# A transformer stack in one kernel: the top-1 expert stages send finished groups home by scatter, with parts of 3 and 5 batches

## The chip, the cores and the metric

The kernel runs on one core of a Trainium2 chip. The metric is the device time of one execution in microseconds (us). TensorE is PE, VectorE DVE, ScalarE ACT, GpSimd POOL and SyncE SP, as in the profile.

## The reference

The input x is 8 batches of 512 tokens of 128 numbers. Eight layers follow each other, each added to x: RWKV mixing, top-1 experts, attention with 16 heads, top-1 experts, attention with a Laplacian function, top-2 experts, Mamba, top-2 experts. The change touches the two top-1 expert layers, which use the same weights:

```python
x = x + _L0_ffn_ref(_layernorm(x, axis=-1), W1, b1, W2, b2, Wr, br)
...
logits = x @ Wr + br                     # 8 experts
idx = jnp.argmax(logits, axis=-1)
probs = jax.nn.softmax(logits, axis=-1)
gates = jnp.take_along_axis(probs, idx[..., None], axis=-1)[..., 0]
for ei in range(e):
    h = jax.nn.gelu(xf @ W1[ei] + b1[ei], approximate=False)
    y = h @ W2[ei] + b2[ei]
    mask = (idxf == ei).astype(xf.dtype)
    out = out + y * (gf * mask)[:, None]
```

W1 is 128 by 512 for each expert and W2 is 512 by 128, all in fp32. Each token uses one expert, chosen by the data.

## The kernel before

x lies in SBUF for the whole program. The stages run one after the other, `STAGES = [RWKV, TOP1, HEADS, TOP1, LAPLACE, TOP2, MAMBA, TOP2]`. At the end of each stage every engine but SP drains and adds to one semaphore, and all wait for the sum of the four (`between`, L1898 to L1901). The order within a stage is written out by hand, engine by engine; semaphores join the engines.

An expert stage (`sorted_tensor`, `sorted_scalar`, `sorted_vector`, `sorted_pool`, `sorted_sync`, L244 to L564) sorts tokens by expert so that each group of 128 rows has one expert. The 8 batches are cut into parts (`PARTS`, L212; for top 1 two parts of 4 batches, 16 tiles of 128 tokens each). For each part:

- DVE takes the statistics (`statistics`), POOL the inverse deviations (L516), DVE normalises into `xn` (L375). PE turns the tiles (L252) and computes the logits (L267), DVE chooses the expert (`route`) and computes each token's place in the sorted order (`places`), with which the index tile is done (L446). A part with n tiles has n + 7 groups, since every expert's rows are rounded up to whole groups; the surplus rows are padding.
- POOL scatters the normalised tiles to the sorted tensor in DRAM by one indirect DMA each (`scatter`, L522).
- SP loads the sorted rows in chunks of up to four groups into a ring of three (`load`, L552). PE turns them; for each group DVE copies the expert's weights (128x1156) into one of five slots (`fill_slot`, L459), PE computes the first layer (L285), ACT the GELU (L329), PE the second layer (L293), and DVE adds b2 into `ys` (`keep`, L466). Part 0 has 23 groups and part 1 too, 46 in all in 12 chunks; they run through in one loop.
- SP stores each finished chunk in sorted order (`store`, L557). When all chunks of a part have landed, POOL gathers each tile of tokens by an indirect DMA (`gather`, L533), and DVE adds it, times its gate, to x (`add`, L474). After batch 0 DVE takes the next stage's first statistics (`take_statistics`). All adds stand behind the whole loop of groups in DVE's order.

When HEADS comes next, ACT ends its part by filling two buffers of that stage with constants (`heads_fill`, L753 and L754), once the last group's second layer is done. POOL ends a stage with the normalisation of the next stage's batch 0 (L172 to L180), unless that is an expert stage.

At the start of the program SP issues the first loads, waits for POOL's `s.filled`, and then issues the loads that later stages need. ACT, also behind `s.filled`, takes one exponential (`decay_scalar`, L1613), on which DVE waits before it mixes RWKV's weights (L1617 to L1624), which PE awaits.

## Time and profile before

| | |
|---|---|
| Median of 3 runs | 2268.59 us (2267.01 to 2269.56) |
| The profiled execution's own time | 2265.75 us |
| Its span | 2264.0 us, mean granted clock 0.828 |
| Busy: PE, DVE, ACT, POOL | 1647.6 (73%), 1665.7 (74%), 1054.8 (47%), 1049.0 us (46%) |
| POOL, indirect scatters `sorted_x<-xn,index` (L522) | 192, busy 195.1 us |
| POOL, indirect gathers `yg<-sorted_y,index` (L533) | 192, busy 194.6 us, idle before them 171.3 us |

A busy time is the sum over instructions. The two indirect lines cover both top-1 stages (32 of each per stage) and both top-2 stages (64 per stage). In a timeline row stand the start, the duration (of the whole run of equal instructions where xN is over 1), the engine and the line; in brackets the idle time before and what ended it.

### The profile page before, as it was taken

To read this page: it belongs to the slowest core of one execution; us is meant where nothing else is said; L and a number is where in the kernel's file an instruction comes from. 1 tells how busy PE (TensorE), PEld (TensorE's weight loads), DVE (VectorE), ACT (ScalarE), POOL (GpSimd) and SP (SyncE) were. 2 spreads that over 40 slices of the span, in tenths; PEclk is the share of its full clock that TensorE was granted. 3 is DMA by queue.
4 is the path that set the end of the run, shared out by engine and by line. 5 is a ranking of instruction groups with operands and counts; after the bars stand their busy time and mean duration, and the time that the engine had idled before them with its cause. 6 is when DMAs were issued, how large, how long until landed. Compare 5 with 4: busy or idle time off the path is not lost. (4 is left out here: it accounts for less than half of the span.)

```text
span 2264.0 us, 28290 instructions
## 1 busy us (share of the span) xinstructions
PE 1647.6 (73%) x8402; PEld 974.4 (43%) x8402; DVE 1665.7 (74%) x3318; ACT 1054.8 (47%) x2009; POOL 1049.0 (46%) x845
## 2 busy tenths in 40 slices
PE   5636935899999985945635943887988888885692
PEld 2326931233333325943435941443443443343692
DVE  7985546888888825546766662899999999997664
ACT  3433640566666771626832632534434444431361
POOL 5636331222222005352207771567666666574776
PEclk8656966999999995977765976988987997896696
DMA  8012315333333201212002530000000000000363
GB/s 248 1 6 69 86 35 63 40 43 45 44 41 44 32 2 46 83 55 61 0 1 76 163 104 33 0 1 1 1 1 0 0 1 0 0 0 12 101 167 107
DMA packets 141594, 102.53 MB, mean 45 GB/s; under 512 B 16360, under 2 KB 133360, under 8 KB 141328
## 3 DMA queue, kind: packets, MB, share of 16 engines
q1 hardware_dynamic: 129168, 75.72, 15.9%
q0 software_dynamic: 12288, 25.19, 3.8%
q8 instruction: 60, 0.98, 0.2%
q14 instruction: 78, 0.64, 0.1%
HBM read 42.92 MB, written 38.27 MB: 36 GB/s over the span
## 5 line engine op out<-in xcount | busy, mean ns | idle before, releaser
L1520 POOL TENSOR_TENSOR m_hc<-m_state,bc 128x512 f32<-128x512 f32 x256 | 378.2, 1477 | 216.9 <-DVE m_state L1463 216.9
L931 DVE TENSOR_REDUCE maxima<-banks 128x1 f32<-128x512 f32 x512 | 320.2, 681 | 46.9 <-PE banks L781 45.8
L1390 ACT ACTIVATE banks<-banks,rates 128x512 f32<-128x512 f32 x256 | 168.8, 661 | 342.7 <-PE banks L1236 342.2
L889 ACT ACTIVATE h_p<-banks 128x512 f32<-128x512 f32 x512 | 274.0, 597 | 113.6 <-PE banks L789 112.5
L1463 DVE TENSOR_TENSOR_SCAN m_state<-banks,m_drive 128x512 f32<-128x512 f32 x256 | 310.1, 1212 | 22.9 <-ACT banks L1390 20.4
L533 POOL DMA_INDIRECT yg<-sorted_y,index x192 | 194.6, 1014 | 171.3 <-DMA sorted_y<-ys 105.3
L329 ACT ACTIVATE hid<-banks,slot 128x128 f32<-128x128 f32 x708 | 211.4, 367 | 110.1 <-PE banks L285 109.8
L522 POOL DMA_INDIRECT sorted_x<-xn,index x192 | 195.1, 1016 | 90.0 <-issue 57.1
L781 PE MATMUL banks<-ks,qs 128*128 128x512 bf16 x512 | 204.8, 402 | 40.8 <-DMA qs<-nothing 22.5
L285 PE MATMUL banks<-xt,slot 128*128 128x128 f32 x1416 | 212.4, 286 | 11.7 <-DVE slot L459 9.8
L293 PE MATMUL banks<-slot,hid 128*128 128x128 f32 x1416 | 201.1, 276 | 0.0
L466 DVE TENSOR_TENSOR ys<-banks,slot 128x128 f32<-128x128 f32 x262 | 76.4, 292 | 162.3 <-PE banks L293 160.3
L789 PE MATMUL banks<-qs,ks 128*128 128x512 bf16 x512 | 191.1, 382 | 4.2 <-ACT h_p L889 2.3
L285 PEld LDWEIGHTS banks<-xt,slot 128*128 128x128 f32 x1416 | 184.6, 198 | 20.7 <-issue 15.9
L1227 PE MATMUL banks<-high,choose 128*128 128x512 f32 x256 | 147.9, 578 | 59.0 <-DVE m_drive L1457 42.0
L293 PEld LDWEIGHTS banks<-slot,hid 128*128 128x128 f32 x1416 | 180.0, 193 | 0.0
L1457 DVE TENSOR_TENSOR m_drive<-banks,bc 128x512 f32<-128x512 f32 x256 | 171.6, 670 | 11.2 <-PE banks L1228 11.1
L984 POOL TENSOR_TENSOR h_less<-less_rest,zero 8x512 bf16<-8x512 f32 x16 | 16.5, 1028 | 327.1 <-DVE less_rest L938 327.1
L321 ACT ACTIVATE xt<-banks 128x512 f32<-128x512 f32 x100 | 58.7, 587 | 216.3 <-PE banks L252 214.7
L1235 PE MATMUL banks<-high,choose 128*128 128x512 f32 x256 | 126.1, 493 | 44.9 <-DVE m_state L1463 44.2
L781 PEld LDWEIGHTS banks<-ks,qs 128*128 128x128 bf16 x512 | 50.0, 98 | 222.2 <-DVE maxima L931 160.6
L798 PE MATMUL banks<-h_p,h_v 128*32 128x512 f32 x1024 | 136.4, 605 | 5.8 <-ACT h_p L889 5.5
(253 smaller groups left out, 3030.6 us busy)
## 6 DMA issues: line engine op xcount, KB each, us to landing
xg<-sorted_x SPq DMA_DIRECT2D x58, 256.0 KB
sorted_y<-ys SPq DMA_DIRECT2D x58, 256.0 KB
qs<-part SPq DMA_DIRECT2D x144, 64.0 KB
ks<-part SPq DMA_DIRECT2D x144, 64.0 KB
sorted_x<-zeros SPq DMA_DIRECT2D x3, 1984.0 KB, 15.6
t1w<-in_t1w SPq DMA_DIRECT2D x16, 256.0 KB, 5.9
sorted_x<-xn,index POOLq DMA_INDIRECT x192, 2.2
yg<-sorted_y,index POOLq DMA_INDIRECT x192
```

Source lines behind the costliest of these rows:

```text
L285: last = pe.matmul(m.bank[2 + g % 3][:, n * P:(n + 1) * P], f.slot[:, g % SLOT_RING, n * P:(n + 1) * P], x, start=True, stop=True)
L293: last = pe.matmul(m.bank[5 + g % 3][:, 0:P], f.hid[:, g % 3, n, :], f.slot[:, g % SLOT_RING, (NB + n) * P:(NB + n + 1) * P], start=n == 0 ...
L329: act.activation(f.hid[:, g % 3, n, :], m.bank[2 + g % 3][:, n * P:(n + 1) * P], f.func, bias=bias).then_inc(f.hidden, 1)
L522: pool.indirect_dma_start(f.xs[p][0:part.groups * P, :], bass.IndirectOffsetOnAxis(ap=f.index[:, v:v + 1], axis=0), f.xn[:, part.tile + n ...
L533: pool.indirect_dma_start(f.yg[:, v, :], None, f.yd[p][0:part.groups * P, :], bass.IndirectOffsetOnAxis(ap=f.index[:, v:v + 1], axis=0)).t ...
L781: pe.matmul(m.bank[bank][:, :], f.qs[:, h, head, tile * P:(tile + 1) * P], f.ks[:, h, head, :], start=True, stop=True).then_inc(f.ring_mad ...
L789: pe.matmul(m.bank[5 + item % SHIFTED_BANKS][:, :], f.ks[:, h, head, tile * P:(tile + 1) * P], f.qs[:, h, head, :], start=True, stop=True) ...
L889: act.activation(f.p[:, slot % 2, j, :], m.bank[5 + item % SHIFTED_BANKS][:, :], ACT.Exp, scale=1.0 / math.sqrt(HD)).then_inc(f.exps, 1)
L931: dve.reduce_max(f.maxima[:, tile, head:head + 1], m.bank[bank][:, :], AX_X).then_inc(f.ring_read, 1)
L1457: dve.tensor_tensor(f.drive[:, n % 4, :], m.bank[4 + n % 2][:, :], f.bc[:, b[1] % 2, 0, :], ALU.mult).then_inc(f.driven, 1)
L1463: dve.tensor_tensor_scan(f.state[:, n % 4, :], m.bank[2 + n % 2][:, :], f.drive[:, n % 4, :], 0.0, ALU.mult, ALU.add).then_inc(f.states, 1)
L1520: pool.tensor_tensor(f.hc[:, n % 8, :], f.state[:, n % 4, :], f.bc[:, now[1] % 2, 1, :], ALU.mult).then_inc(f.weighed, 1)
```

## The change

The top-1 stages (`f.back` = 1) work as follows; the top-2 stages keep their way.

- A row of the sorted tensor has 129 numbers: the 129th is the token's number as an integer. POOL makes the numbers once (`m.ids`); at the stage's head DVE copies them behind the rows of `xn`. The scatter carries them along. Each use has row tensors of its own in DRAM, filled at the start with padding rows: ACT writes a zero block `m.pads`, POOL numbers it from 4096 on, and SP stores it four times, behind `s.filled` 2.
- When a chunk is there, DVE copies its numbers into `f.home`, 128x4 (`noted`). A later load into the same place of the ring waits for that too.
- `ys` has room for all 46 groups. As soon as a group is kept, POOL scatters it to `m.home`, in the tokens' order (`send_back`). When all groups of a part are sent, SP loads its batches plainly (`fetch`), up to three at a time.
- Parts have 3 and 5 batches (19 and 27 groups). DVE adds part 0's batches after group 40 of 46 (`EARLY_ADDS` = 6), with the next stage's first statistics, and part 1's after the loop.
- The masks for `places` now exist for four sizes instead of two. In the head stage one semaphore takes the place of another.

```diff
 EXPERTS = 8
-PARTS = {1: (4, 4), 2: (2, 3, 3)}
+PARTS = {1: (3, 5), 2: (2, 3, 3)}
+ROW = P + 1
+EARLY_ADDS = 6
 STEPS = {(1, 2): 42, (2, 3): 107}
-CONSTANTS = 5
-HEADS_GAP = 3392
+CONSTANTS = 7
+HEADS_GAP = 3096
 SLOT_RING = 5
...
         activate(g)
     if f.fill:
         act.wait_ge(f.second, f.base.second + len(f.groups))
+        act.wait_ge(f.noted, f.base.noted + len(f.chunks) * f.back)
         for p, part in enumerate(f.parts):
             act.wait_ge(f.scattered[p], f.base.scattered[p] + 16 * part.lanes)
         heads_fill(act, m, f.fill)
...
     def keep(g):
         c, t = f.groups[g]
-        if t == 0 and c >= 3:
+        if f.back and t == 0:
+            chunk = f.chunks[c]
+            dve.wait_ge(f.loaded[c % 3], f.base.loaded[c % 3] + 16 * (c // 3 + 1))
+            dve.tensor_copy(f.home[:, g:g + chunk.size], f.xg[:, c % 3, 0:chunk.size, P].bitcast(U32)).then_inc(f.noted, 1)
+        if not f.back and t == 0 and c >= 3:
             dve.wait_ge(f.stored[c % 3], f.base.stored[c % 3] + 16 * (c // 3))
+        y = f.ys[:, g, :] if f.back else f.ys[:, c % 3 * 4 + t, :]
         dve.wait_ge(f.second, f.base.second + g + 1)
-        dve.tensor_tensor(f.ys[:, c % 3, t, :], m.bank[5 + g % 3][:, 0:P], f.slot[:, g % SLOT_RING, 2 * NB * P + NB:], ALU.add).then_inc(f.kept, 1)
+        dve.tensor_tensor(y, m.bank[5 + g % 3][:, 0:P], f.slot[:, g % SLOT_RING, 2 * NB * P + NB:], ALU.add).then_inc(f.kept, 1)
     def add(part, b):
-        dve.wait_ge(f.gathered[b % 4], f.base.gathered[b % 4] + 16 * TILES * K * (b // 4 + 1))
+        if f.back:
+            dve.wait_ge(f.stored[b % 3], f.base.stored[b % 3] + 16 * (b // 3 + 1))
+        else:
+            dve.wait_ge(f.gathered[b % 4], f.base.gathered[b % 4] + 16 * TILES * K * (b // 4 + 1))
         for k in range(K):
             for t in range(TILES):
                 v = part.lane + k * part.tiles + (b - part.first) * TILES + t
...
                 steps.done(last)
         last.then_inc(f.added, 1)
+    def add_part(part):
+        for b in part.batches:
+            add(part, b)
+            if b == 0 and not last_stage:
+                dve.wait_ge(f.added, f.base.added + 1)
+                ahead = Steps(dve, f.ahead_steps, 3)
+                ahead.begin((0, f.turn))
+                take_statistics(dve, nc, m, s, (0, BATCHES), stage, ahead)
+
+    if f.back:
+        dve.tensor_copy(f.xn[:, :, P].bitcast(U32), m.ids[:, :])
     statistics(f.parts[0])
     normalise_part(0, f.parts[0])
     for p, part in enumerate(f.parts):
@@ -494,14 +517,10 @@
         keep(g)
         if more:
             fill_slot(g + 4, expert)
-    for part in f.parts:
-        for b in part.batches:
-            add(part, b)
-            if b == 0 and not last_stage:
-                dve.wait_ge(f.added, f.base.added + 1)
-                ahead = Steps(dve, f.ahead_steps, 3)
-                ahead.begin((0, f.turn))
-                take_statistics(dve, nc, m, s, (0, BATCHES), stage, ahead)
+        if f.back and g == len(f.groups) - EARLY_ADDS:
+            add_part(f.parts[0])
+    for part in f.parts[f.back:]:
+        add_part(part)
     assert steps.n - f.base.steps == STEPS[K, len(f.parts)], steps.n - f.base.steps
...
         for n in range(part.lanes):
             v = part.lane + n
             pool.indirect_dma_start(f.xs[p][0:part.groups * P, :], bass.IndirectOffsetOnAxis(ap=f.index[:, v:v + 1], axis=0),
-                                    f.xn[:, part.tile + n % part.tiles, :], None).then_inc(f.scattered[p], 16)
+                                    f.xn[:, part.tile + n % part.tiles, 0:f.row], None).then_inc(f.scattered[p], 16)
     def gather(p, part):
         chunks = sum(q.chunks for q in f.parts[:p + 1])
...
                 pool.indirect_dma_start(f.yg[:, v, :], None, f.yd[p][0:part.groups * P, :],
                                         bass.IndirectOffsetOnAxis(ap=f.index[:, v:v + 1], axis=0)).then_inc(f.gathered[b % 4], 16)
+    def send_back(g):
+        c, t = f.groups[g]
+        pool.wait_ge(f.noted, f.base.noted + c + 1)
+        pool.wait_ge(f.kept, f.base.kept + g + 1)
+        pool.indirect_dma_start(m.home[:, :], bass.IndirectOffsetOnAxis(ap=f.home[:, g:g + 1], axis=0),
+                                f.ys[:, g, :], None).then_inc(f.scattered[f.chunks[c].p], 16)
+
     inverse_deviations(0, f.parts[0])
     for p, part in enumerate(f.parts):
         if p + 1 < len(f.parts):
             inverse_deviations(p + 1, f.parts[p + 1])
         scatter(p, part)
-    for p, part in enumerate(f.parts):
-        gather(p, part)
+    if f.back:
+        for g in range(len(f.groups)):
+            send_back(g)
+    else:
+        for p, part in enumerate(f.parts):
+            gather(p, part)
 def sorted_sync(sp, nc, m, s, f):
...
             sp.wait_ge(f.scattered[chunk.p], f.base.scattered[chunk.p] + 16 * chunk.part.lanes)
         if c >= 3:
             sp.wait_ge(f.turned, f.base.turned + BATCHES + c - 2)
-        sp.dma_start(f.xg[:, c % 3, 0:chunk.size, :], chunk.rows(f.xs[chunk.p])).then_inc(f.loaded[c % 3], 16)
+        if f.back and c >= 3:
+            sp.wait_ge(f.noted, f.base.noted + c - 2)
+        sp.dma_start(f.xg[:, c % 3, 0:chunk.size, 0:f.row], chunk.rows(f.xs[chunk.p])).then_inc(f.loaded[c % 3], 16)
     def store(c):
         chunk = f.chunks[c]
         sp.wait_ge(f.kept, f.base.kept + sum(other.size for other in f.chunks[:c + 1]))
-        sp.dma_start(chunk.rows(f.yd[chunk.p]), f.ys[:, c % 3, 0:chunk.size, :]).then_inc(f.stored[c % 3], 16)
+        sp.dma_start(chunk.rows(f.yd[chunk.p]), f.ys[:, c % 3 * 4:c % 3 * 4 + chunk.size, :]).then_inc(f.stored[c % 3], 16)
+
+    def fetch(p, b):
+        sp.wait_ge(f.scattered[p], f.base.scattered[p] + 16 * (f.parts[p].lanes + f.parts[p].groups))
+        if b >= 3:
+            sp.wait_ge(f.stored[b % 3], f.base.stored[b % 3] + 16 * (b // 3))
+        sp.dma_start(f.yg[:, b * TILES:(b + 1) * TILES, :], m.home[b * S:(b + 1) * S, :].rearrange("(t p) d -> p t d", p=P)).then_inc(f.stored[b % 3], 16)
     for c in range(3):
         load(c)
     for c in range(len(f.chunks)):
         if c + 3 < len(f.chunks):
             load(c + 3)
-        store(c)
+        if not f.back:
+            store(c)
+    if f.back:
+        for p, part in enumerate(f.parts):
+            for b in part.batches:
+                fetch(p, b)
 def experts_pool(pool, nc, m, s, f, stage):
...
+        back = [Part(0, batches, 1).groups for batches in PARTS[1]]
+        m.rows = [[nc.dram_tensor(f"rows{use}_{p}", (groups * P, ROW), F32) for p, groups in enumerate(back)] for use in range(stages.count(TOP1))]
+        m.home = nc.dram_tensor("home", ((BATCHES * TILES + sum(back)) * P, P), F32)
+        m.ids = sb("ids", [P, BATCHES * TILES], U32)
         m.constants = sem("m_constants")
         s = Names()
...
+                    m.pads = into(own)("pads", [P, sum(back), ROW])
+                    for rows_of_use in m.rows:
+                        loads += [(rows_of_part[:, :].rearrange("(t p) d -> p t d", p=P), m.pads[:, sum(back[:p]):sum(back[:p + 1]), :])
+                                  for p, rows_of_part in enumerate(rows_of_use)]
                     plans[stages.index(RWKV)] = (f, rwkv_tensor, rwkv_scalar, rwkv_vector, rwkv_pool)
             if HEADS in stages:
                 with ExitStack() as own:
...
-            sp.wait_ge(s.filled, 1)
+            sp.wait_ge(s.filled, 2)
             for tile, dram in loads:
                 sp.dma_start(tile, dram).then_inc(s.loaded, 16)
             if late_loads and late == 0:
...
             act.wait_ge(s.filled, 1)
+            act.activation(m.pads[:, :, 0:P], m.zeros[:, :].unsqueeze(1).to_broadcast([P, sum(back), P]), ACT.Copy).then_inc(s.filled, 1)
             credit(act, s.xt, 1)
             for do in setup.scalar:
                 do(act)
...
             pool.memset(m.zeros[:, :], 0.0)
+            pool.iota(m.ids[:, :], [[P, BATCHES * TILES]], 0, 1)
+            pool.iota(m.pads[:, :, P].bitcast(U32), [[P, sum(back)]], BATCHES * S, 1)
             pool.memset(m.pair[:, :], ONE_PAIR)
             pool.memset(m.xt[:, :, 0:1], 0.0).then_inc(s.filled, 1)
```

POOL, the first TOP1 stage, before: the last scatters, then the gathers (`yg`) of part 0 and of part 1's first batches.

```order
L522 DMA sorted_x<-xn,index 2944x128 [waits moe_indexed]
L522 DMA sorted_x<-xn,index 2944x128 x15
L533 DMA yg<-sorted_y,index 128x128 [waits moe_stored2,moe_stored1,moe_stored0]
L533 DMA yg<-sorted_y,index 128x128 x15
L533 DMA yg<-sorted_y,index 128x128 [waits moe_stored2,moe_gathered0,moe_stored1,moe_stored0]
L533 DMA yg<-sorted_y,index 128x128 x3
L533 DMA yg<-sorted_y,index 128x128 [waits moe_gathered1]
```

The same place with the change:

```order
L541 DMA rows_0<-xn,index 2432x129 [waits moe_indexed]
L541 DMA rows_0<-xn,index 2432x129 x11
L541 DMA rows_1<-xn,index 3456x129 [waits moe_indexed]
L541 DMA rows_1<-xn,index 3456x129 x19
L559 DMA home<-ys,home 9984x128 [waits moe_kept,moe_noted] x46
```

All 46 sends of groups (`home<-ys,home`, one row) stand behind all scatters, and no gather is left; part 0 has 12 scatters and part 1 has 20.

DVE, the same stage, groups 40 and 41 of 46, before (`ys` is a group's sum, `slot` the weights of the group four further on; ISA rows are register work):

```order
L466 TENSOR_TENSOR ys<-banks,slot 128x128 [waits moe_second]
L459 ISA [waits moe_kept,moe_second]
L459 COPY slot<-t1w 128x1156
L453 TENSOR_LOAD owner
L453 ISA x2
L466 TENSOR_TENSOR ys<-banks,slot 128x128 [waits moe_second]
L459 ISA [waits moe_kept,moe_second]
L459 COPY slot<-t1w 128x1156
```

With the change (`x<-yg,gate,x` are the adds, four to a batch; the first statistics of the next stage follow batch 0's):

```order
L475 TENSOR_TENSOR ys<-banks,slot 128x128 [waits moe_second]
L463 ISA [waits moe_kept,moe_second]
L463 COPY slot<-t1w 128x1156
L486 SCALAR_TENSOR_TENSOR x<-yg,gate,x 128x128 [waits moe_stored0]
L486 SCALAR_TENSOR_TENSOR x<-yg,gate,x 128x128 x3
L155 BN_STATS bn<-x 128x6 [waits s_normed,moe_added]
...
L486 SCALAR_TENSOR_TENSOR x<-yg,gate,x 128x128 [waits moe_stored1]
L486 SCALAR_TENSOR_TENSOR x<-yg,gate,x 128x128 x3
L486 SCALAR_TENSOR_TENSOR x<-yg,gate,x 128x128 [waits moe_stored2]
L486 SCALAR_TENSOR_TENSOR x<-yg,gate,x 128x128 x3
...
L475 TENSOR_TENSOR ys<-banks,slot 128x128 [waits moe_second]
...
L463 COPY slot<-t1w 128x1156
```

Between group 40's slot copy and group 41's sum there now lie twelve adds and the statistics; the copy for the last slot (L463, last row) is behind them.

ACT, the start of the program, before:

```order
L1963 UNCONDITIONAL_BRANCH [waits barrier_Pool_Activation_PE_DVE_SP_release]
L1613 ACT_TABLE_LOAD [waits s_first_loaded,s_filled]
L1613 ACTIVATE decay<-decay 128x1
L196 ACTIVATE xt<-banks 128x512 [waits s_transposed,rwkv_decayed]
L628 ACTIVATE rwkv_k<-banks 128x512 [waits rwkv_kvr]
```

With the change:

```order
L2020 UNCONDITIONAL_BRANCH [waits barrier_Pool_Activation_PE_DVE_SP_release]
L2024 ACT_TABLE_LOAD [waits s_filled]
L2024 ACTIVATE pads<-zeros 128x46x128 [waits s_first_loaded]
L1655 ACTIVATE decay<-decay 128x1
L197 ACTIVATE xt<-banks 128x512 [waits s_transposed,rwkv_decayed]
L671 ACTIVATE rwkv_k<-banks 128x512 [waits rwkv_kvr]
```

The padding block `pads` is written between the table load and the exponential `decay`.

## Rows read from the trace of the kernel before

**Rows 1.** Windows view: window, length, busy us (count) of PE, PEld, DVE, ACT, POOL, clock, DMA, GB/s
```profile
299.00:331.00 32.00, 0.00 (x0) 0.00 (x0) 11.12 (x42) 13.34 (x2) 18.52 (x20) 0.56 0.15 39
```

**Rows 2.** Timeline of DVE, first TOP1 stage: start us, us, engine, line, operation, [idle before <-releaser]
```profile
157.36 3.17 DVE L361 BATCH_NORM_STATS2 bn<-x 128x6 f32<-128x128 f32 x16
...
176.04 0.29 DVE L396 TENSOR_TENSOR lg<-banks,t1br 128x128 f32<-128x128 f32 x1 [3.21 <-PE banks L267]
...
183.01 0.17 DVE L446 CAST index<-dest 128x16 uint32<-128x16 f32 x1
...
202.30 0.17 DVE L446 CAST index<-dest 128x16 uint32<-128x16 f32 x1
...
204.03 3.15 DVE L459 COPY slot<-t1w 128x1156 f32 x4 [1.06 <-issue]
...
298.61 1.13 DVE L474 SCALAR_TENSOR_TENSOR x<-yg,gate,x 128x128 f32<-128x128 f32 x4
...
301.45 3.23 DVE L474 SCALAR_TENSOR_TENSOR x<-yg,gate,x 128x128 f32<-128x128 f32 x12
```

**Rows 3.** Timeline of POOL, the same stage
```profile
161.60 2.90 POOL L516 TENSOR_TENSOR rstd<-var,minus_half 128x16 f32<-128x16 f32 x1 [14.38 <-DVE var L370]
...
183.49 1.20 POOL L522 DMA_INDIRECT sorted_x<-xn,index  x1 [7.68 <-DVE index L446]
...
202.77 0.96 POOL L522 DMA_INDIRECT sorted_x<-xn,index  x1 [0.30 <-issue]
...
260.66 0.98 POOL L533 DMA_INDIRECT yg<-sorted_y,index  x1 [33.86 <-DMA sorted_y<-ys]
...
282.45 1.41 POOL L533 DMA_INDIRECT yg<-sorted_y,index  x1 [0.30 <-issue]
302.26 0.94 POOL L533 DMA_INDIRECT yg<-sorted_y,index  x1 [18.40 <-DMA sorted_y<-ys]
...
321.00 0.94 POOL L533 DMA_INDIRECT yg<-sorted_y,index  x1 [0.30 <-issue]
```

**Rows 4.** Timeline of PE, the same stage
```profile
188.52 1.09 PE L252 MATMUL banks<-ident,xn 128*128 128x128 f32 x4
...
190.97 1.09 PE L252 MATMUL banks<-ident,xn 128*128 128x128 f32 x4
...
209.74 4.96 PE L285 MATMUL banks<-xt,slot 128*128 128x128 f32 x24
...
239.97 0.49 PE L252 MATMUL banks<-ident,xg 128*128 128x128 f32 x3
...
295.52 2.84 PE L293 MATMUL banks<-slot,hid 128*128 128x128 f32 x24
```

**Rows 5.** Timeline of ACT, end of the same stage
```profile
298.40 7.03 ACT L753 ACTIVATE qs<-zeros 64x8192 f32<-64x8192 f32 x1 [1.53 <-PE banks L293]
305.33 7.01 ACT L754 ACTIVATE ks<-pair 64x8192 f32<-64x8192 f32 x1
```

**Rows 6.** Timelines where the stages meet (stage 1 to 2, 2 to 3, 3 to 4)
```profile
323.63 2.13 DVE L474 SCALAR_TENSOR_TENSOR x<-yg,gate,x 128x128 f32<-128x128 f32 x4 [3.97 <-DMA yg<-sorted_y,index]
...
330.83 0.51 POOL L1003 MEMSET nothing<- 4x512 bf16 x1 [5.48 <-POOLq L1900]
...
847.98 3.19 DVE L361 BATCH_NORM_STATS2 bn<-x 128x6 f32<-128x128 f32 x16 [0.26 <-DVEq L1900]
...
1020.66 0.87 DVE L154 BATCH_NORM_STATS2 bn<-x 128x6 f32<-128x128 f32 x4 [5.11 <-POOLq L1900]
```

**Rows 7.** Timeline, start of the program
```profile
7.69 1.11 POOL L172 TENSOR_TENSOR rstd<-mean_var,minus_half 128x4 f32<-128x4 f32 x1 [1.49 <-DVE mean_var L164]
7.82 0.15 DVE L1617 TENSOR_SCALAR decay<-decay 128x1 f32<-128x1 f32 x1 [0.21 <-ACT decay L1613]
```

**Rows 8.** DMA issues of the whole program: KB each, median us from issue to landing
```profile
sorted_x<-xn,index POOLq DMA_INDIRECT x192, 2.2
...
x<-in_x SPq DMA_DIRECT2D x8, 256.0 KB, 4.1
```

39 lines of the change are left out of this document (23 added, 16 removed).

## The prediction, made before the changed kernel was run

> **What bounds the kernel now.** I first cut the span into its eight stages and read the windows view. PE, DVE and POOL each lead somewhere, so no mean share helps; what counts is each stage's own end. In the first TOP1 stage the last 32 us have no matmul at all, while POOL is busy for 18.52 of them [rows 1]. The timelines of that stage then give its chain in four pieces.
>
> Piece 1, routing: DVE starts at 157.36 with its statistics, waits 3.21 for PE's logits, and has part 0's indices at 183.18; part 1's come at 202.47 [rows 2]. Piece 2, scatter: POOL issues 16 scatters, the first at 183.49, the last at 202.77, so 1.285 each; PE's first expert layer comes 6.97 after the start of the last one, at 209.74 [rows 3, 4]. Piece 3, the 46 groups: 209.74 to 298.36, 88.6 us, PE being fed without gaps [rows 4]. Piece 4, the way home: the last chunk is stored, POOL waits until 302.26 and issues 16 gathers, the last at 321.00 (1.249 each); DVE's last add ends at 325.76, and the next stage begins at 330.83 [rows 3, 6]. This last gap is the barrier: the row at 330.83 waited 5.48 for POOL's own queue, so POOL's drain, 9.83 after the start of its last indirect DMA, is what ends the stage. Where POOL had no such DMAs, the next stage waited only 0.26 [rows 6]. The second TOP1 stage repeats this: 847.98 to 1020.66 is 172.7 us, against 157.36 to 330.83, 173.5 us [rows 2, 6].
>
> **Routing and first scatter (parts of 3 and 5 batches).** One batch through PE's turns and logits takes 2.45 [rows 4]. Part 0 loses one: 2.45, plus 1.3 from four tiles fewer (a quarter of 3.17 in DVE's statistics and, as an estimate, 0.5 of POOL's 2.90 for the deviations [rows 2, 3]), plus some 0.5 from narrower passes, so its indices come 4.3 earlier, at 178.9. Twelve scatters of 1.285 instead of 16: the last starts at 179.2 + 11 x 1.285 = 193.3, and by the 6.97 above the first layer could run at 200.3. But slots come later in DVE's order: part 1 has one batch more, so its indices and the four slot copies move by only -4.4 + 2.45 + 0.6 = -1.3. The first copy starts at 202.7, takes 0.79 [rows 2], and PE starts at **203.5 instead of 209.74, -6.2**. The bare copy of token numbers at the stage's head is one pass over 32 elements, taken at 0.1.
>
> **The 46 groups.** The number of groups (19 + 27) and of chunks (12) is unchanged, so 88.6 us stay, ending at 292.1. Two things can add. First, part 1's 20 scatters follow its indices: 201.3, eight at the calm 1.285, twelve at the rate that POOL shows beside DVE's slot copies, (282.45 + 1.41 - 260.66) / 16 = 1.45 [rows 3]; POOL is free at 229.0, the last having started at 227.5. PE turns part 1's first chunk 30.2 after its first layer (239.97 against 209.74 [rows 4]), now 233.7; the chunk needs the 2.2 landing [rows 8] and a load. I take 0, bounds 0 and 3. Second, DVE now adds part 0's three batches after keeping group 40: 1.13 for the first four tiles, 1.71 for the next stage's statistics, two thirds of 3.23 for the rest [rows 2], 5.0 in all. Slot 45 is copied behind that, some 6.9 after group 40's sum is ready, while PE wants it after four layers of about 0.9. PE stalls 3.3: the last layer ends at **295.5**, the last keep at 295.8. So nearly half of the earlier start is given back. The twelve copies of token numbers (128x4) lie in DVE's idle time (a group takes 88.6 / 46 = 1.93, its slot copy 0.79 and its sum some 0.3 of that); without this cover they would cost at most 12 x 0.2. Loads of later chunks also wait for them; they are issued three chunks ahead, and the work of a chunk covers that.
>
> The rows are 516 bytes instead of 512. I take no cost: POOL's issue, not the transfer, paces the scatters. No row here can show it.
>
> **The way home.** Gone are 12 stores on SP and 32 gathers on POOL; in come 46 sends, one for each group, then 8 plain loads on SP. POOL starts sending at 229.0 with ten groups waiting. At 1.45 each it would be through at 229.0 + 66.7 = 295.7, while the last group is kept at 295.8: POOL catches up just in time. The last send starts at 296.0 and lands 2.2 later [rows 8], at 298.2. Part 0's loads are long done. Part 1's: three are issued at once, the other two wait for the first two to land. With 4.1 for a 256 KB load in a stream of eight [rows 8], the last lands about 298.2 + 4.1 + 4.1 + 0.5 = 306.9, its add ends at 308.0, and 0.26 later the stage may end: **308.3**. POOL's drain, 9.83 after its last send, is over at 305.8, under this cover; if loads landed faster, 305.8 would be the next limit.
>
> In the first TOP1 stage ACT is later still. It fills the head buffers only once the last layer is done: 13.94 us [rows 5], so far hidden behind the gathers (312.34 against 330.83). Now 295.5 + 13.94 + 0.5 = 310.0, and this ends the stage: **-20.8** against 330.83. The second TOP1 stage has no fill; its length becomes 308.3 - 157.36 = 150.9 against 172.7: **-21.8**.
>
> **The start.** The two TOP1 uses have own row tensors, whose padding rows must carry numbers. ACT writes this block, 46 x 128 elements per partition, ahead of the exponential on which DVE waits at once (0.21 idle, released by ACT [rows 7]); DVE then mixes the weights PE waits for. From 8192 elements in 7.03 [rows 5], 5888 take 5.05, all on the path. ACT also waits for POOL's two number passes. No row has such a pass: below 0 they can't be, since ACT waits for them; above, two at POOL's arithmetic pass of 1.11 [rows 7] are 2.2. I take 0.8, nearer to the plain writes that they resemble. **+5.9**, bounds 5.0 and 7.3. The first-stage loads start as much later and carry 6 MB more, under 157 us of the first stage; two more masks on DVE (about 0.5) lie there too, beside a wait for x.
>
> **Sum.** -20.8 - 21.8 + 5.9 = -36.7. The profiled execution took 2265.75 (span 2264.0); it stands 2.84 under the median of 2268.59. 2265.75 - 36.7 = 2229.05, and on the median's footing **2231.9**.
>
> **Rivals.** (a) POOL doesn't catch up. If a send takes 1.6 beside the slot copies, POOL is through at 302.6 instead of 297.0: 5.6 more in the second stage, 3.9 in the first (313.9 against ACT's 310.0). 2241.4. For it: single operations there take 1.41 + 0.30 [rows 3], and 46 in a row leave no pause; against it: the mean of 16 is 1.45. Chance 0.20.
> (b) The fill at the start is not on the path, because the first stage takes up its shift elsewhere. 2226.0. Against it speaks the 0.21 wait [rows 7]; chance 0.12.
> (c) Slower: POOL is shut out by the slot copies. If each send had to wait for a whole copy first, it would take 1.25 + 0.79 = 2.04, POOL would be through at 229.0 + 93.8 = 322.8, 25.8 later; the first stage would lose 24.1 of its gain, the second all of 25.8, and the kernel would take 2281.8. The point from which this mechanism makes the change a loss is 1.90 per send. The gathers beside the same copies took 1.45, so chance 0.04. The Trainium skill (SBUF — State Buffer, SBUF: two separate sides) has this rule: while DVE copies fp32 in its two-port mode, POOL cannot write its DMA descriptors at all. The trace agrees with a delay, not with a full one per send (1.45 against 1.249).
> (d) The change doesn't do what it says: a tail remains because each stage still ends on POOL's drain, now longer with 46 sends behind it. At 5 us more per stage, drains end at 310.8: +0.8 and +2.5, 2235.2. Chance 0.06.
> The forecast itself has 0.52; 0.05 is for gains beyond it (no stall from the early adds where DVE is faster, 2 x 3.3) and 0.01 for no difference.
>
> **Numbers.** A measurement of this kernel can tell about 0.2%, 4.5 us, from no change. All cases but (c) and the last one are faster by more: 0.95 faster, 0.01 same, 0.04 slower. The range takes in the bounds of the start (-0.9, +1.4), the late chunk (+6), no stall (-6.6) and cases (a), (b) and (d), and leaves out (c): 2222 to 2245.
>
> **What would show it.** Right: PE's first expert layer about 46 us after the first statistic, not 52.4; a PE stall near group 45 of 3.3; POOL's sends back to back until 296 at some 1.45; ACT's second fill as the last work before the first TOP1 stage ends; ACT's padding write of 5.05 before the decay. Wrong: sends over 1.6, a first wait of PE on part 1's chunk, a barrier of 5 us after the last add, or DVE's wait at the start no longer than 0.21.

## The result, and the profile after

The changed kernel takes 2231.5 us, median of 4 runs (2230.0 to 2234.4), against 2267.8 for the kernel before (4 runs, 2265.8 to 2269.6): the ratio is 0.984, 95% interval 0.983 to 0.986. The forecast was 2231.9. The profiled execution took 2230.0, with a span of 2228.0, 36.0 less than the span before.

The stages, measured to the first instruction behind the barrier, the first TOP1 stage from its first statistic (DVE), the second from DVE's first instruction in it (in the changed kernel the copy of the token numbers, 0.1 ahead of the statistic):

| | before | forecast | after |
|---|---|---|---|
| first statistic of the first TOP1 stage, at | 157.36 | +5.9 | 161.46, +4.1 |
| first TOP1 stage | 173.5 | -20.8 | 154.3, -19.2 |
| second TOP1 stage | 172.7 | -21.8 | 153.0, -19.7 |
| behind it, to the end of the span | 1243.3 | same | 1242.6 |

So the sum was nearly exact and its terms were less so, which is in part luck: the start cost 1.8 less than forecast, and each TOP1 stage gave 1.6 to 2.1 less. The start first, timelines of ACT, DVE and PE in the changed kernel, columns as in [rows 7]:

```profile
8.10 5.12 ACT L2024 ACTIVATE pads<-zeros 128x5888 f32<-128x5888 f32 x1
13.12 0.18 ACT L1655 ACTIVATE decay<-decay 128x1 f32<-128x1 f32 x1
...
13.33 0.15 DVE L1659 TENSOR_SCALAR decay<-decay 128x1 f32<-128x1 f32 x1 [5.52 <-ACT decay L1655]
...
14.31 0.68 DVE L1666 TENSOR_SCALAR w_now<-w_now,mix 128x128 f32<-128x128 f32 x3
...
15.05 1.11 PE L190 MATMUL banks<-ident,xn 128*128 128x128 f32 x4 [15.05 <-DVE w_now L1666]
```

DVE waits 5.52 where it waited 0.21 [rows 7]. But PE begins only 4.0 later than before (11.08 there): the mixing of w_now takes 0.68 for its three instructions, while before it took 2.23, at a time when POOL was normalising. In the changed kernel POOL is through with that at 11.2, before DVE mixes. The write itself was 5.12 against 5.05 forecast.

The first TOP1 stage, timelines of DVE, PE, POOL and ACT (one after the other), the last row being the next stage's first instruction:

```profile
161.46 2.40 DVE L365 BATCH_NORM_STATS2 bn<-x 128x6 f32<-128x128 f32 x12
...
207.61 4.58 PE L288 MATMUL banks<-xt,slot 128*128 128x128 f32 x24 [3.00 <-DVE slot L463]
...
239.51 0.66 PE L255 MATMUL banks<-ident,xg 128*128 128x128 f32 x4 [2.00 <-DMA xg<-rows]
...
297.86 1.13 PE L288 MATMUL banks<-xt,slot 128*128 128x128 f32 x8 [3.37 <-issue]
298.83 2.84 PE L296 MATMUL banks<-slot,hid 128*128 128x128 f32 x24
...
233.57 0.96 POOL L541 DMA_INDIRECT rows<-xn,index  x1 [0.30 <-issue]
234.84 1.08 POOL L559 DMA_INDIRECT home<-ys,home  x1 [0.30 <-issue]
...
294.32 0.96 POOL L559 DMA_INDIRECT home<-ys,home  x1 [0.31 <-issue]
297.84 0.96 POOL L559 DMA_INDIRECT home<-ys,home  x1 [2.57 <-DVE ys L475]
...
303.50 0.96 POOL L559 DMA_INDIRECT home<-ys,home  x1 [0.30 <-issue]
...
308.64 7.01 ACT L797 ACTIVATE ks<-pair 64x8192 f32<-64x8192 f32 x1
...
308.49 5.38 DVE L486 SCALAR_TENSOR_TENSOR x<-yg,gate,x 128x128 f32<-128x128 f32 x20 [6.49 <-DMA yg<-home]
...
315.74 0.52 POOL L1046 MEMSET nothing<- 4x512 bf16 x1 [8.02 <-ACTq L1957]
```

PE's first layer comes 46.15 after the first statistic (forecast 46.1, before 52.4). Two stalls of PE follow: 2.00 on part 1's first chunk, and 3.37 behind the early adds, where the slot of group 45 was late (its copy starts at 297.01 and takes 0.75). In the second TOP1 stage the stall behind the adds is 3.36, and on part 1's first chunk only 0.3. POOL sends back to back: 40 steps from 234.84 to 294.32, 1.49 each; then it waits 2.57 for DVE, whose adds hold up the keeping of group 41. ACT's second fill ends at 315.65 and the next stage begins at 315.74: the fill ends this stage, as forecast.

The second TOP1 stage (832.43 to 985.41), PE, POOL and DVE at its end:

```profile
968.53 4.47 PE L296 MATMUL banks<-slot,hid 128*128 128x128 f32 x24
...
974.19 0.96 POOL L559 DMA_INDIRECT home<-ys,home  x1 [0.30 <-issue]
...
982.90 2.19 DVE L486 SCALAR_TENSOR_TENSOR x<-yg,gate,x 128x128 f32<-128x128 f32 x8 [0.35 <-DMA yg<-home]
...
985.41 0.87 DVE L155 BATCH_NORM_STATS2 bn<-x 128x6 f32<-128x128 f32 x4 [0.32 <-DVEq L1957]
```

Its barrier waits 0.32, for DVE's last add, where [rows 6] have 5.11 for POOL's drain. The last three groups' layers take 4.47 here and 2.84 in the first TOP1 stage, the same 24 matmuls. The windows view of these stretches (columns as in [rows 1]) says why:

```profile
299.00:302.00 3.00, 2.67 (x24) 2.48 (x23) 0.88 (x3) 1.44 (x5) 1.91 (x2) 1.00 0.13 44
...
967.50:973.00 5.50, 5.43 (x32) 5.27 (x32) 0.83 (x4) 1.14 (x4) 2.94 (x4) 0.69 0.11 36
```

Behind a stall of 3.4 the granted clock stayed at 1.00 (2.4 GHz) once, and once fell towards half (1.2 GHz), with a mean of 0.69. What decides between the two, no run here shows.

### The profile page after: what moved, and what is told of

It is laid out like the page before. It is cut to its first block and busy times, and to the rows that moved or that the text cites. A ratio compares the mean times of both kernels' runs of the same rounds, so it can differ in the third digit from the quotient of the medians.

```text
span 2228.0 us, 28443 instructions
## 1 busy us (share of the span) xinstructions
PE 1651.1 (74%) x8402; PEld 976.7 (44%) x8402; DVE 1663.3 (75%) x3348; ACT 1060.0 (48%) x2010; POOL 1089.6 (49%) x875
## 5 line engine op out<-in xcount | busy, mean ns | idle before, releaser
L1499 DVE TENSOR_TENSOR m_drive<-banks,bc 128x512 f32<-128x512 f32 x256 | 171.3, 669 | 11.2 <-PE banks L1270 11.0
L541 POOL DMA_INDIRECT sorted_x<-xn,index x128 | 127.1, 993 | 55.7 <-issue 38.2
L324 ACT ACTIVATE xt<-banks 128x512 f32<-128x512 f32 (+1 forms) x100 | 58.7, 587 | 199.9 <-PE banks L255 198.7
L552 POOL DMA_INDIRECT yg<-sorted_y,index x128 | 127.2, 994 | 48.6 <-issue 45.7
```

Source lines behind the costliest of these rows:

```text
L1499: dve.tensor_tensor(f.drive[:, n % 4, :], m.bank[4 + n % 2][:, :], f.bc[:, b[1] % 2, 0, :], ALU.mult).then_inc(f.driven, 1)
```

## Experiments

All times are medians. Twelve kernels were measured, on four chips, each beside the kernel before. Its median there was 2267.8 (experiment 1, late adds with parts of 3 and 5, decay first), 2266.6 (late adds with parts of 4 and 4, split pads, 516-byte rows, two-source copies), 2265.6 (zero from PSUM and the two kernels with early slots next to it) and 2264.5 (the last one). So two times from different chips are compared by their ratios to the kernel before. The columns are the two TOP1 stages' lengths in the profiled execution, the time, and this ratio:

| | first | second | time | ratio |
|---|---|---|---|---|
| before | 173.5 | 172.7 | 2267.8 | 1 |
| parts 3 and 5, gathers | 172.6 | 172.2 | 2267.0 | 1.0002 |
| parts 4 and 4, sends | 162.5 | 160.2 | 2245.2 | 0.9895 |
| **the change: parts 3 and 5, sends** | 154.3 | 153.0 | 2231.5 | 0.9842 |
| gathers, 516-byte rows | 174.4 | 173.5 | 2264.6 | 0.9990 |
| decay first | 157.7 | 152.9 | 2230.1 | 0.9832 |
| late adds | 150.6 | 151.5 | 2228.3 | 0.9834 |
| late adds, parts 4 and 4 | 155.7 | 154.9 | 2237.3 | 0.9862 |
| late adds, two-source copies | 164.2 | 166.7 | 2255.4 | 0.9955 |
| late adds, split pads | 151.7 | 152.4 | 2223.8 | 0.9805 |
| the same, zero from PSUM | 150.6 | 151.0 | 2224.2 | 0.9821 |
| the same, early slots | 149.5 | 149.4 | 2221.9 | 0.9802 |
| split pads, early slots, fast copies | 151.1 | 151.9 | 2221.6 | 0.9812 |
| **split pads, early slots, all slots with the zero from PSUM** | 147.8 | 147.9 | 2219.0 | 0.9800 |

The part behind the second TOP1 stage, which no edit touches, takes 1240.5 to 1247.3 in these profiles. So a difference of a few us between two kernels is read from the stages, and only confirmed by the times. The stages vary as well. In the kernels with parts of 3 and 5, the fast copies and the first slots behind part 1's indices, PE's stall on part 1's first chunk was anything from none to 2.1, although what they do in the stage up to there differs only in the way home and the rows' length: 2.00 and 0.3 in the change's two stages, none and 1.32 with gathers, 0.32 and 1.39 with late adds, 2.11 and 0.2 with decay first, 1.74 and 1.43 with split pads. A difference in length under 2 us therefore counts only where the rows show where it comes from.

**1. Which half of the change works.** The changed kernel with the old parts:

```diff
-PARTS = {1: (3, 5), 2: (2, 3, 3)}
+PARTS = {1: (4, 4), 2: (2, 3, 3)}
```

> The changed kernel, but with its parts in the top-1 stages of 4 and 4 batches again. Theory (the two halves of the change work through different pieces): PE's first expert layer comes some 6 us later than in the changed kernel (about 52 after the stage's first DVE statistic, not 46.15); the stall of 2.4 on part 1's first chunk goes, since the chunk then has 23 groups ahead of it instead of 19 and 16 scatters instead of 20; the early adds of 4 batches take 6.1 instead of 5.0, so their stall grows by 1.1. Last keep +6.2 - 2.4 + 1.1 = +4.9 in each top-1 stage, of which the second gets 1 to 2 back from one load fewer for part 1. Time about 2231.5 + 4.9 + 3.4 = 2240. Rival (the unequal parts do nothing, the way home gives all): 2232 +- 2. Rival (nearly all comes from the parts): over 2255.

Measured: 2245.2, ratio to before 0.990 (0.987 to 0.992). The four executions lie apart (2239.6, 2241.3, 2249.1 and 2249.9), and the profile is of the 2249.1. There is no stall on part 1's first chunk, as expected. PE's first layer came 53.3 after the first statistic, where 52 was expected, and the stages are 8.2 and 7.2 longer than the change's, not 4.9 and 3.4. Most of the missing part of the first stage stands at the end, first PE's timeline, then the window behind it:

```profile
303.12 2.05 PE L288 MATMUL banks<-xt,slot 128*128 128x128 f32 x8 [4.40 <-issue]
304.96 4.80 PE L296 MATMUL banks<-slot,hid 128*128 128x128 f32 x24
...
304.00:310.00 6.00, 5.76 (x30) 5.57 (x29) 0.79 (x3) 1.35 (x5) 2.32 (x4) 0.58 0.10 33
```

The stall is 4.40 and the clock behind it 0.58, so the last layers take 2.05 + 4.80 where the change's first stage has 1.13 + 2.84. In the second stage, behind a stall of 4.40 too, they take 2.05 + 3.43.

The other half, the kernel before with parts of 3 and 5 and its stores and gathers:

```diff
-PARTS = {1: (4, 4), 2: (2, 3, 3)}
+PARTS = {1: (3, 5), 2: (2, 3, 3)}
```

> The kernel before with parts of 3 and 5 batches alone; stores and gathers stay. Theory: PE's first expert layer comes 6 us earlier (46 after the stage's first statistic), but part 1 now has 20 gathers behind the last store instead of 16, 4 x 1.25 = 5.0 more on the path, and part 1's first chunk stalls PE by up to 2.4: -6.2 + 5.0 + (0 to 2.4) = -1.2 to +1.2 in each of the two stages, 2265 to 2270: no change that can be measured. So the parts would pay only together with the sends. Rival (the halves simply add up): whatever the first experiment of this call leaves for the parts, some 8 us, is found here too: 2259.

Measured: 2267.0, ratio 1.000 (0.999 to 1.002). PE's first layer did come at 46.2, and the last keep 5.6 earlier than before's. Then 20 gathers lie on the path instead of 16, and the stages are 0.9 and 0.5 shorter. So the halves don't add up: parts alone 0.8 us, sends alone 22.6, parts beside sends 13.7. Of these 13.7 a part is the clock behind the early adds; experiment 2 takes it out.

**2. The early adds.** Part 0's adds behind the last group:

```diff
-        if f.back and g == len(f.groups) - EARLY_ADDS:
-            add_part(f.parts[0])
-    for part in f.parts[f.back:]:
+    for part in f.parts:
         add_part(part)
```

> The changed kernel with part 0's adds behind the last group instead of behind group 40. Theory A (the early adds cost more than they save, since DVE idles behind the last keep): PE's stall of 3.6 near group 45 goes, the last keep comes at about 298 instead of 301.7, the last send starts at POOL's own pace of 1.44, about 299.7 instead of 303.5; DVE does part 0's adds (5.0) from 298 to 303, while the sends end and the loads fly, and part 1's from about 305 on. In the first top-1 stage ACT's fill starts and ends 3.6 earlier, 312.1: -3.6; in the second the loads come 3.8 to 4.2 earlier: -4. Time 2231.5 - 7.6 = 2224. Rival B (the adds belong where they are, DVE's tail is the limit): part 0's adds of 5.0 come in front of part 1's, and nothing is won in the second stage: 2228 to 2233.

Measured: 2228.3, stages of 150.6 and 151.5, so -3.7 and -1.5. In the first stage, PE, POOL and DVE:

```profile
294.06 2.84 PE L296 MATMUL banks<-slot,hid 128*128 128x128 f32 x24
...
301.25 1.08 POOL L557 DMA_INDIRECT home<-ys,home  x1 [0.30 <-issue]
...
306.54 5.34 DVE L486 SCALAR_TENSOR_TENSOR x<-yg,gate,x 128x128 f32<-128x128 f32 x20 [4.26 <-DMA yg<-home]
```

PE's stall is gone (last layers from 294.06 instead of 298.83) and DVE idles 4.26 before part 1's rows even with the adds late: theory A. Of the 4.8 by which the last layers come earlier, only 3.4 are this stall; the rest is mostly the smaller stall on part 1's first chunk, 0.32 instead of 2.00, which no edit here causes. In the second stage that stall goes the other way (1.39 instead of 0.3), and still the last keep comes 4.7 earlier. But in the first stage the last send comes only 2.3 earlier, 4.3 behind the last keep (296.94): now POOL is the bound, at 1.49 per send, and in the second stage, where the last send comes only 1.5 earlier, that takes back most of the gain. The next stage then waited for POOL's drain, not for ACT. The ratio, 0.9834 (0.9812 to 0.9856), can't be told from the change's 0.9842.

With late adds, parts of 4 and 4:

> The changed kernel with late adds and parts of 4 and 4. With early adds the equal parts gave first top-1 stages of 162.5 and 160.2 instead of 154.3 and 153.0; PE stood still for 4.4 behind the adds, and its granted clock was then at half (0.58 from 304 to 310). Theory (of that +8 and +7, the adds' stall and the lower clock behind it are 4 to 5 each, the later first layer the rest): without the stall the clock stays at 1.00 to the last layer; first layer +7, no stall on part 1's first chunk -2; last keep some 4.5 later than in the late-adds kernel with 3 and 5, but one load and one add fewer behind it: stages of 155 and 153.5, 2235. Rival (the clock falls anyway at the end, or the equal parts are worse for another reason): stages of 160 and more, 2243.

Measured: 2237.3, stages of 155.7 and 154.9, PE's clock 1.00 to the last layer (296 to 304). So of the first experiment's stages, 6.8 and 5.3 are what early adds of four batches cost, stall and clock together; parts of 3 and 5 are worth 8.5 us beside late adds by the stages (5.1 and 3.4), and some 6 by the ratios (0.9834 against 0.9862).

**3. The start.** The exponential first, the write behind it:

```diff
-            act.activation(m.pads[:, :, 0:P], m.zeros[:, :].unsqueeze(1).to_broadcast([P, sum(back), P]), ACT.Copy).then_inc(s.filled, 1)
             credit(act, s.xt, 1)
             for do in setup.scalar:
                 do(act)
+            act.activation(m.pads[:, :, 0:P], m.zeros[:, :].unsqueeze(1).to_broadcast([P, sum(back), P]), ACT.Copy).then_inc(s.filled, 1)
```

> The changed kernel with ACT's exponential of the decay ahead of its write of the padding block, all else the same. Theory: DVE's wait at the start falls from 5.52 to some 0.5 and its mixing begins at about 8.4; POOL's normalising passes then run beside it again, so w_now takes 2.2 instead of 0.68, and PE's first transpose comes at about 11.6 instead of 15.04. But ACT is in its write until about 13.4 and keeps the first transposed tile only then, not at 12.8: about 0.6 back. -2.8 at the first top-1 stage's start, and the time 2228.7. Rival (the first stage swallows a shift of its start): first stage no shorter, 2231.5. Rival (loads held back by the write set the end of the first stage): the same, since the write ends when it did.

Measured: the first TOP1 stage starts at 158.49 instead of 161.46, -3.0. The time, 2230.1, doesn't show it clearly: it is 1.4 below the change's, where 2.8 were expected. The profiled execution took 2235.6, the longest of five; its first TOP1 stage is 3.4 longer than the change's, by another fall of the clock behind the early adds (0.54 from 295.5 to 302, the last 24 matmuls take 4.78). Without early adds, and with the write in two pieces (SP's wait for `s.filled` then goes to 3):

```diff
+            act.activation(m.pads[:, 0:34, 0:P], m.zeros[:, :].unsqueeze(1).to_broadcast([P, 34, P]), ACT.Copy).then_inc(s.filled, 1)
...
             keep_transposed(act, nc, m, s, new, stage)
+        if new and not now:
+            act.activation(m.pads[:, 34:46, 0:P], m.zeros[:, :].unsqueeze(1).to_broadcast([P, 12, P]), ACT.Copy).then_inc(s.filled, 1)
```

> The changed kernel with late adds; and at the start ACT does the exponential of the decay first, then writes 34 of the 46 padding tiles (4352 elements, about 3.8 us), keeps the first transposed tile, and then writes the other 12 (1.3 us) while PE multiplies. Theory: nothing of the write is left on the path, PE's first transpose at 12.0 as with the decay first and ACT ready for it (the 1.02 wait of PE back to 0.75); the first top-1 stage starts at about 158.1 instead of 161.5, so the time is 3.4 below the late-adds kernel: 2225. Rival: the first stage takes up the shift elsewhere, 2228.

Measured: 2223.8, ratio 0.9805, against 0.9834 with late adds alone; the first TOP1 stage starts at 158.50 instead of 161.66. The RWKV stage doesn't swallow this shift. The two TOP1 stages are 1.1 and 0.9 longer in this profile, the stalls on part 1's first chunk being 1.74 and 1.43, and the other stages 3.5 shorter, so the time alone would not prove the 3.2.

**4. Rows of 516 bytes.** The kernel before, with rows of 129 elements:

```diff
+    if f.row > P:
+        dve.memset(f.xn[:, :, P], 0.0)
...
-            f.xs, f.yd = m.xs, m.yd
+            f.xs, f.yd, f.row = (m.rows, m.yd, P + 1) if top == 1 else (m.xs, m.yd, P)
...
-                f.xn = tile(f"xn{n}", [P, tiles, P])
+                f.xn = tile(f"xn{n}", [P, tiles, f.row])
```

> The kernel before (parts of 4 and 4, stores and gathers), but the top-1 stages scatter and load rows of 129 elements, 516 bytes, the last element a zero; nothing uses it. In the changed kernel with parts of 4 and 4, PE's first expert layer came 53.3 after the stage's first statistic, in the kernel before 52.4, and from the start of part 0's last scatter to PE's turn of the first chunk it was 6.1 against 5.15. Theory A (rows of 516 bytes are slower through the DMA engines): those 53.3 and 6.1 are found here, 0.9 more per top-1 stage, and about 2 us in all: 2270. Theory B (the rows' length costs nothing, the 0.9 has another cause): 52.4 and 5.15, 2268.

Part 0's last scatter and PE's turn of the first chunk:

```profile
202.97 0.95 POOL L524 DMA_INDIRECT rows<-xn,index  x1 [0.30 <-issue]
...
209.07 1.97 PE L252 MATMUL banks<-ident,xg 128*128 128x128 f32 x8 [10.07 <-DMA xg<-rows]
```

6.10, against 5.15 in the kernel before (202.77 [rows 3] to its turn at 207.92), and the first layer at 53.3: theory A. In the second stage the first chunk's turn comes 5.21 behind the last scatter (before 5.11), but the second chunk's turn then waits 0.44, and the first layer is 0.85 later all the same. Both stages are 0.8 to 0.9 longer. The time, 2264.6, doesn't show it (ratio 0.999, 0.998 to 1.000, where 2 us more would be 1.001).

**5. What slows POOL.** Slot copies by an instruction with two sources:

```diff
-        dve.tensor_copy(f.slot[:, g % SLOT_RING:g % SLOT_RING + 1, :], f.w[:, bass.ds(expert, 1), :]).then_inc(f.slots, 1)
+        slot, w = f.slot[:, g % SLOT_RING:g % SLOT_RING + 1, :], f.w[:, bass.ds(expert, 1), :]
+        if f.back and g >= 4:
+            dve.scalar_tensor_tensor(slot, w, 1.0, w, ALU.mult, ALU.max).then_inc(f.slots, 1)
+        else:
+            dve.tensor_copy(slot, w).then_inc(f.slots, 1)
```

> The changed kernel with late adds, and the slot copies of groups 4 to 45 in the top-1 stages made by a DVE instruction with two tensor sources (the weights times one, larger of it and the weights: the same values), which takes about 1.2 us instead of 0.75. Theory A (what makes POOL's sends 1.49 instead of 1.26 is DVE's fast copy, which holds the port that POOL writes descriptors through): scatters and sends of the loop go at 1.26, the stall on part 1's first chunk goes, POOL catches up with PE before the last group, the last send starts some 0.5 after the last keep; last send 4 to 5 earlier than in the late-adds kernel. The first stage is then bound by ACT's fill (-2.5), the second top-1 stage by the loads and adds (-4.5): 2221. Theory B (any DVE instruction between buffers of the same memory delays POOL, in proportion to its length): each copy holds POOL longer, a send takes 1.6 to 1.7, the last one starts 6 us or more later: 2240 or more. Theory C (DVE becomes the bound: 0.29 + 1.2 + the register load in 1.79): PE's groups take longer than 1.79, each 0.1 costs 4 us per stage.

Measured: 2255.4, ratio 0.9955, against 0.9834 with fast copies, and stages 13.6 and 15.2 longer; 40 sends take 1.71 each, PE stalls 5.38 on part 1's first chunk. Theory A falls in this form: a copy by this instruction is slower for POOL, not faster. Next, on top of the split padding writes, the second source from PSUM (a column of zeros, in a bank that PE is not writing then):

```diff
+            zero = m.bank[5 + (g - 4) % 3][:, 511:512].unsqueeze(1).to_broadcast([P, 1, 2 * NB * P + NB + P])
-            dve.scalar_tensor_tensor(slot, w, 1.0, w, ALU.mult, ALU.max).then_inc(f.slots, 1)
+            dve.scalar_tensor_tensor(slot, w, 1.0, zero, ALU.mult, ALU.add).then_inc(f.slots, 1)
```

> The kernel with late adds and split padding writes (2223.8), and the slot copies of groups 4 to 45 made by the weights times one plus a zero that is read from PSUM: one tensor from SBUF, one from PSUM, about 1.35 us each like the instruction with both sources in SBUF, which made POOL's steps in the loop 1.73 instead of 1.49. Theory A (POOL is kept out by the second read path to SBUF, which that instruction and the fast copy both use; a length of 1.35 by itself does no harm): POOL's steps go at 1.26 to 1.3 beside these copies, the stall of 1.7 on part 1's first chunk shrinks to under 0.5, POOL catches up with PE and the last send starts within 1 us of the last keep, 4 us earlier; the first top-1 stage is then bound by ACT's fill (-1.5), the second by loads and adds (-4): 2218. Theory B (any DVE instruction keeps POOL out for its length): 1.73 per step as before, some 2253.

Groups view, 240 to 290, POOL's sends with both sources in SBUF, then with one in PSUM:

```profile
L561 POOL DMA_INDIRECT home<-ys,home x30 | 42.9, 1428 | 9.1 <-issue 7.3 <-DVE ys L479 1.8
...
L564 POOL DMA_INDIRECT home<-ys,home x31 | 29.7, 957 | 19.5 <-DVE ys L480 15.2 <-issue 4.0 <-DVE home L475 0.3
...
L466 DVE SCALAR_TENSOR_TENSOR slot<-t1w,banks 128x1156 f32<-128x1156 f32 x27 | 36.4, 1348 | 0.0
```

Copies of the same 1.35 us, and a send takes 0.96 beside one kind and 1.43 beside the other. POOL now waits for the sums (15.2), part 1's first chunk comes without a stall, and the last send is at 296.31 instead of 299.28. The stages are 1.1 and 1.5 shorter, less than expected in the second, and the time, 2224.2, doesn't show it; the part behind them was 3.6 longer in this profile. PE's rows tell why the stages gain so little. From the first layer to the start of the last second layers' run it takes 87.57 here and 87.44 with fast copies, though the latter include the stall of 1.74. Here 25 steps from the start of one layer to the next take 0.96 to 1.19 instead of 0.89; with fast copies, apart from the stall, none takes over 0.90. DVE is busy for 1.35 + 0.29 of each 1.79 now, so the likely reason, not tested by itself, is that slots come late by a little: theory C of the expectation for the copies with two SBUF sources. POOL's gain is paid for in PE's loop.

The Trainium skill (SBUF — State Buffer, SBUF: two separate sides) says that GpSimd is locked out by a DVE instruction in a two-port mode, and by one with two SBUF inputs where the GpSimd instruction reads SBUF. The runs agree with both: 1.49 per send beside the fast copy, 1.71 beside two SBUF sources, 0.96 + 0.30 beside one SBUF and one PSUM source. (A send has its index tile in SBUF.)

**6. Early slots.** PE waited 3.00 for its first slot, while DVE had been idle for 8.7 before part 1's routing:

```diff
+        if p == 0 and f.back:
+            for g in range(4):
+                fill_slot(g, expert_of(g))
-    for g in range(4):
+    for g in range(4 * (1 - f.back)):
         fill_slot(g, expert_of(g))
...
     def second_layer(g):
+        if g == 0 and f.back:
+            pe.wait_ge(f.indexed, f.base.indexed + len(f.parts))
```

> As the run with the zero from PSUM, and the slots of groups 0 to 3 are copied in DVE's idle 8.7 us between its normalising of part 1 and part 1's routing, instead of behind part 1's indices; PE's second layer of group 0 waits for part 1's indices, which costs nothing by the trace. Theory: PE's wait of 3.0 for the first slot goes, the first layer comes about 43 after the stage's first statistic instead of 46.15; part 1's scatters end where they did, so part 1's first chunk stalls PE by 1 to 3 again and takes part of it back. If POOL goes at 1.26 to 1.3: -1 to -2 per top-1 stage against the run before; if POOL goes at 1.73, it is the bound, and nothing is won.

> As the run with early slots, but with the fast copies as in the changed kernel (late adds, split padding writes). Theory: PE's first layer at about 43 after the first statistic instead of 46.15, but POOL is the bound of both top-1 stages there (66 operations of some 1.49 from part 1's indices on, last send 4 behind the last keep), and its start does not move: the stall on part 1's first chunk grows from 1.7 to some 4.7, the last send comes when it did, and the time stays at 2223.8 +- 2. Rival (PE's start is worth its 3.0 in each stage): 2218.

Measured: 2221.9 and 2221.6. The first layer came at 45.6 and 45.8, not 43: the four fast copies fell among POOL's scatters of part 0. POOL and DVE in the second TOP1 stage of the first of these two kernels:

```profile
851.00 3.59 POOL L551 DMA_INDIRECT rows<-xn,index  x1 [0.30 <-issue]
...
850.99 2.77 DVE L470 COPY slot<-t1w 128x1156 f32 x4
```

Beside four fast copies without a pause between them, one scatter takes 3.59 instead of 0.96: it ends 0.83 behind the last copy. The other three stages of the two kernels show the same, 3.57 or 3.58. In the first stage of the first kernel the last scatter of part 0 started at 196.70, in the next kernel at 194.07. With fast copies throughout almost nothing is gained, as its theory said: the stages are 151.1 and 151.9, against 151.7 and 152.4 with split pads alone, and the last send comes 140.1 after the first statistic, there 140.8. The next kernel gives these four slots, too, the zero from PSUM (the condition on g goes):

> As the run with early slots and the zero from PSUM, but groups 0 to 3 too take their slots by the instruction that reads the zero from PSUM (4 x 1.35 in DVE's idle 8.7). With the fast copies there, PE turned the first chunk 3 us later than without early slots (43.8 after the stage's first statistic against 40.9), and the first layer came only at 45.6. Theory (the four fast copies held up part 0's scatters on POOL): the first chunk is turned at 40.9 again, the first layer comes at about 43.0, part 1's first chunk stalls PE by about 1; both top-1 stages about 1.5 shorter than the 149.5 and 149.4 of the run before: 148, and the time 2219. Rival (the scatters are late for another reason, DVE's presence alone): 45.6 again and no gain.

```profile
199.47 2.00 PE L255 MATMUL banks<-ident,xg 128*128 128x128 f32 x8 [1.52 <-DMA xg<-rows]
...
232.11 0.66 PE L255 MATMUL banks<-ident,xg 128*128 128x128 f32 x4 [0.38 <-DMA xg<-rows]
```

Measured: first layer at 201.28, 43.0 after the first statistic; a stall of 0.38 on part 1's first chunk; stages of 147.8 and 147.9; 2219.0 (2217.3 to 2221.9), ratio to before 0.980 (0.978 to 0.982). It is 45.5 below the kernel before on its chip, where the change was 36.3 below on its own. By its stages this is the best version found; by its time it can't be told from the kernel with early slots before it (0.9802).

## Why the prediction came out right, step by step

- **Routing and first scatter**: 46.1 forecast, 46.15 measured; PE waited for the slot, as said. Right.
- **The 46 groups, part 1's first chunk**: "I take 0, bounds 0 and 3". It was 2.00 in the first stage and 0.3 in the second, inside the bounds. In the first, 20 scatters went at a mean of 1.48 (205.41 to 233.57 is 19 steps) instead of a mix of 1.285 and 1.45, which is 1.38, and the way from the last one to the chunk's turn was 5.94, not the 5.15 of the kernel before. Neither size is fixed by the code: over the stages of the kernels with the same parts and fast copies the mean is 1.41 to 1.49 and this way, where PE waits for it, 5.26 to 7.46. The kernel before with parts of 3 and 5 and 512-byte rows shows the same spread, no stall in its first stage and 1.32 in its second. What decides it stays open.
- **Early adds**: 3.3 forecast, 3.37 measured. Right in the first stage. In the second (3.36) the clock fell behind it, 1.6 on the last layers (4.47 against 2.84), which the prediction had no term for. I also had not asked whether the adds belong there at all.
- **POOL's rate**: 1.45 forecast, 1.49 measured. "POOL catches up just in time" held, and only because the early adds delayed the last sums. Without them POOL is 4.3 behind: rival (a) is what bounds the late-adds kernel.
- **The end**: the first stage ended by ACT's fill, right; its last keep came 140.25 after the first statistic, forecast 138.4. In the second the last send came 141.8 after the stage's start (forecast 138.6), the last add ended 10.9 after the send's start (forecast 12.0): the loads fed the adds with one gap of 0.35.
- **The start**: +5.9 forecast, +4.1 measured. The write was sized right; the two number passes cost 0.3 together instead of 0.8, and the 1.55 that DVE saved by mixing without POOL beside it was overlooked. The DMA that all engines wait for first landed 0.2 later. Rival (b) falls: experiment 3 gets 3.0 back.
- **Rival (c)**, a loss: no. Its mechanism is real (experiment 5), its price not: a copy takes 0.75 in each 1.79, so it holds up some sends by 0.5, and not each by a whole copy. The whole lock that this rival feared shows where copies follow without a pause: 3.57 for one scatter (experiment 6).
- **Rival (d)**: the drain ended 10.7 after the last send's start (303.50 to 314.2) instead of 9.83, under cover of the fill. As a price, no; as the next bound, yes: it ended the first stage once the adds were late.
In the kernel before the runs show 0.9 per stage: the page was right there, and my reason ("POOL's issue, not the transfer, paces") overlooked the one load that PE waits for. In the changed kernel the 0 held all the same, by luck: its first layer waits for the slot, not for the load, and came at 46.15 where it came at 46.16 with rows of 512 bytes (experiment 1).

In sum: the start was 1.8 better than forecast and the two stages 3.7 worse, which leaves -34.8; the stage between them and the part behind, taken as unchanged, were 0.5 and 0.7 shorter, which makes -36.0. The mechanism came out as forecast; that the sum did to within 1 us is luck, since errors of 1.8 and 3.7 had opposite signs and 1.2 came from stages that no edit touches.

## What to carry to other kernels

When a step is taken off the end of a stage, list all that ends within a few us of it (here fill, drain, last send, last add), since the next edit's gain is the distance to the second of these. Put work where an engine is idle only after asking what it locks or delays there: the same adds, and the same slot copies, gained or lost by their place and by the ports they used. And two edits that each shorten a different piece of one chain are worth most together: the unequal parts gave 0.8 us alone and, beside the sends, 13.7 with early adds and 6 to 9 with late ones.
